# Loads of x from the fifth group on started by ScalarE instead of SyncE

## The reference, cut to what matters

```python
x = x + 0.5 * ffn(layernorm(x))        # ffn: fft over the 512 channels, sparse complex weights, inverse fft, bias
x = x + attn(layernorm(x))             # attn: layernorm, a long causal convolution over time (s4d), residual,
                                       #       layernorm, fc1, gelu, fc2, residual
x = x + 0.5 * ffn(layernorm(x))
```

## Time and profile before

| what | value |
|---|---|
| time, median of 3 runs | 2082.71 us (2082.7, 2082.71, 2084.4) |
| time of the profiled execution | 2079.76 us |
| its span (first to last instruction) | 2078.0 us |
| PE busy | 1893.0 us (91%) |
| DVE busy | 1390.8 us (67%) |
| POOL busy | 970.0 us (47%) |
| ACT busy | 918.9 us (44%) |
| DMA | 210.63 MB, mean 101 GB/s |
| mean granted TensorE clock | 0.97 of full |

### The profile page before, as it was taken

The page is one execution under the profiler, slowest core; times in us unless marked ns, Lnnn a source line. Parts: engine busy times, 40 slices in busy tenths (PEclk is TensorE's granted clock), DMA queues, the critical chain, the costliest instruction groups (busy, mean ns, idle before and its releaser), DMA issues.

```text
span 2078.0 us, 34662 instructions
## 1 busy us (share of the span) xinstructions
PE 1893.0 (91%) x12416; PEld 1185.6 (57%) x12416; DVE 1390.8 (67%) x2456; ACT 918.9 (44%) x1509; POOL 970.0 (47%) x690
## 2 busy tenths in 40 slices
PE   7866677589966999999999999999999999999999
PEld 6433333267645576665756657475665757656574
DVE  4777899867884667656566665657666566665663
ACT  3555677855654243332433424253342424433250
POOL 0665777654443353443535434353543425444351
PEclk9988999889987999999999999999999999999999
DMA  7154233249994223143232323323132232313321
GB/s 254 61 220 177 110 121 122 69 136 283 262 348 119 56 62 67 51 77 97 62 62 57 76 57 78 82 62 63 56 78 65 74 77 62 70 48 77 76 41 41
DMA packets 282956, 210.63 MB, mean 101 GB/s; under 512 B 193058, under 2 KB 227490, under 8 KB 280995
## 3 DMA queue, kind: packets, MB, share of 16 engines
q1 hardware_dynamic: 282788, 208.35, 36.0%
HBM read 103.97 MB, written 66.56 MB: 82 GB/s over the span
## 4 chain that ended last, share of the span: by engine, by line
PE 75%; DVE 9%; DMA 5%; issue 5%; POOL 2%; ACT 2%; SPq 1%; DVEq 0%; ACTq 0%; POOLq 0%
PE psum L1888 32%; PE psum L1844 28%; PE psum L1751 8%; DMA arena<-in_x 3%; PE psum L1802 3%; PE psum L1793 1%; PE psum L1714 1%; DVE bn L1173 1%; DVE arena L1335 1%; DVE bn L1343 1%; PE psum L1811 1%; DVE ring L1389 1%; SPq L496 1%; DVE taps L1307 1%; POOL arena L662 1%
## 5 line engine op out<-in xcount | busy, mean ns | idle before, releaser
L1888 PE MATMUL psum<-arena 128*128 128x512 f16 x3072 | 668.3, 379 | 0.0
L1844 PE MATMUL psum<-arena 128*128 128x256 f16 x5376 | 599.5, 274 | 43.7 <-DMA arena<-taps 33.3
L1844 PEld LDWEIGHTS psum<-arena 128*128 128x128 f16 x5376 | 525.8, 98 | 120.7 <-issue 45.7
L1888 PEld LDWEIGHTS psum<-arena 128*128 128x128 f16 x3072 | 300.3, 98 | 355.9
L1751 PE MATMUL psum<-m_parts,taps 128*128 128x512 f16 x1536 | 354.1, 386 | 80.3 <-DVE taps L1307 78.7
L766 POOL TENSOR_SCALAR arena<-ring,sc 128x512 f16<-128x512 f32 x192 | 297.9, 1563 | 158.5 <-ACT ring L1016 153.1
L642 POOL TENSOR_TENSOR va<-va,mhalf 128x4 f32<-128x4 f32 x79 | 86.7, 1101 | 546.4 <-DVE va L1166 530.5
L1751 PEld LDWEIGHTS psum<-m_parts,taps 128*128 128x128 f16 x1536 | 149.4, 99 | 259.4 <-issue 95.6
L1030 ACT ACTIVATE ring<-psum 128x256 f32<-128x256 f32 x96 | 36.8, 383 | 362.9 <-PE psum L1844 352.6
L1609 DVE SCALAR_TENSOR_TENSOR arena<-ring,sc,arena 128x512 f16<-128x512 f32 x192 | 177.5, 924 | 11.8 <-POOL arena L766 11.8
L766 POOL TENSOR_SCALAR arena<-spare,sc 128x512 f16<-128x512 f32 x64 | 99.2, 1562 | 182.5 <-ACT spare L1016 180.5
(11 more groups left out here) (193 smaller groups left out, 2423.1 us busy)
## 6 DMA issues: line engine op xcount, KB each, us to landing
arena<-in_x SPq DMA_DIRECT2D x16, 1024.0 KB, 9.8
x_scratch<-arena SPq DMA_DIRECT2D x16, 1024.0 KB, 4.3
taps<-taps_copies SPq DMA_DIRECT2D x64, 256.0 KB, 4.1
y_scratch<-arena SPq DMA_DIRECT2D x32, 512.0 KB, 6.0
arena<-y_scratch SPq DMA_DIRECT2D x15, 1024.0 KB, 5.8
arena<-x_scratch SPq DMA_DIRECT2D x15, 1024.0 KB, 5.5
out<-arena SPq DMA_DIRECT2D x15, 1024.0 KB, 4.4
taps<-taps_copies SPq DMA_DIRECT2D x64, 128.0 KB, 4.4
```

The costliest lines, as they stand in the source:

```text
L1844: last = pe.matmul(chain(p), w1_sb[i][:, a, k, p * P:(p + 1) * P], gt[:, 4 * i + 2 * b + k, :], start=start and n == 0, stop=stop and n == ...
L1888: last = pe.matmul(bank(4 + j % 2), hid[:, a, hc, j * P:(j + 1) * P], w2_sb[:, b, hc, :], start=(p == 0 and not lower and n == 0), stop=(p ...
```

## The change

The `load` function of SyncE is gone, with its calls; the two instructions that were in it besides the waits are now issued by ScalarE, directly behind line 927 of a group's fourth tile, for groups 0 to 11. ScalarE waits for its own `u_norm` of that tile, adds to `gate`, waits for the landing of the group's store, and starts the load of the group four later into the same buffer. SyncE keeps its stores and its copies of the taps, which now follow each other with only the wait for `x1_ready` between them.

```diff
-            def load(g, quad, q):
-
-                sp.wait_ge(u_norm, 4 * g)
-                sp.sem_inc(gate, 1)
-                sp.wait_ge(x1_stored[(q - 1) % 4], 16 * ((quad if q else quad - 1) + 1))
-                sp.dma_start(xbuf[(q - 1) % 4], rows(x, g + 3)).then_inc(x_loaded[(q - 1) % 4], 16)
-
             sp.wait_ge(taps_stored, 32)
             store(0, 0, 0)
             copy_taps(0)
             for g in range(1, 4):
                 store(g, 0, g)
-                load(g, 0, g)
                 copy_taps(g)
             with sp.Fori(1, QUADS - 1) as quad:
                 for q in range(4):
                     store(4 * quad + q, quad, q)
-                    load(4 * quad + q, quad, q)
             store(GROUPS - 4, QUADS - 1, 0)
-            load(GROUPS - 4, QUADS - 1, 0)
...
                     act.activation(uring[:, t.j, :], xbuf[t.q][:, t.j, :], ACT.Identity,
                                    scale=va[:, 7, t.j:t.j + 1], bias=ubias[:, t.j:t.j + 1]).then_inc(u_norm, 1)
+                    if t.j == GT - 1 and not (isinstance(t.g, int) and t.g + 4 >= GROUPS):
+                        act.wait_ge(u_norm, 4 * t.g + 4)
+                        act.sem_inc(gate, 1)
+                        act.wait_ge(x1_stored[t.q], 16 * t.quad + 16)
+                        act.dma_start(xbuf[t.q], rows(x, t.g + 4)).then_inc(x_loaded[t.q], 16)
```

## The result

| | before | after |
|---|---|---|
| median of 12 runs each | 2082.69 us | 2078.34 us |
| profiled execution: span | 2078.0 us | 2074.0 us |

The ratio of after to before is 0.9982, with a 95% interval of 0.9973 to 0.999: a gain of 3.7 us, between 2.1 and 5.6. The interval excludes 1, and the gain is just under the 0.2% that the prediction took as its bound. The forecast was 2082.2, a gain of 0.5. Three executions further down were far slower than the rest of their kernel (4999 us of `copy_first`, 2829 us of `pad_act`, 9155 us of `after_sp_equal`, whose only trace is of that one), and no ratio counts them.

A forecast was written before the change was run, and what follows sets the result against it. Four DMA engines serving copy, store and load one after the other were taken to bound the first half. Terms -0.5 + 0 on 2079.76 gave 2079.3; with the median 2.95 us higher, the forecast was 2082.2 us, range 2073 to 2090.

The forecast's parts named there:

- Four engines bound the first half: Taps copies, 115 to 230 us: four DMA engines serve copy, store and load in turn; DVE waits 31.3 us.
- Piece by piece, so 0.5 us a landing and not adding up: Four slow loads: engines alternate queues one piece at a time; each lands 0.5 us sooner, gains not adding up.
- SyncE's part costs and gives nothing; copy 1's issue becomes short: SyncE loses twelve loads: gain nothing, as nobody waits for it; copy 1 follows store 1 at 119.8 us, issue short.
- ScalarE's step, 0.7 us under a cover of 1.56: ScalarE behind line 927: wait, count, registers and issue cost 0.7 us twelve times, hidden in 1.56 us idle; term 0.
- Sum, -0.5 us: Whole launch: -0.5 + 0 on an execution of 2079.76 us gives 2079.3; forecast median 2082.2 us.
- the change does not touch it: Last stage, 1438 of 2078.0 us: unaffected by the change; x stage shifts reach the launch's end one for one.
- Rival one: Taps copies: load passes the copy, DVE's waits go, ScalarE waits for stores; 8.4 us gained, 2074.3; chance 0.23.
- Rival two: Taps copies: copy passes the load, first landing near 167 us; +13 us, 2095.7; chance 0.11.
- Rival three: ScalarE's wait and issue exceed 1.56 us of cover; at 2.1 us the price is 6 us, 2088.7; chance 0.11.
- Rival four: DMA engines serve one transfer's whole share before changing queues; each load lands 2.55 us sooner, 2080.1; chance 0.12.
- within 0.2%: Whole launch: time changes by no more than 0.2%, 4.2 us, indistinguishable from no change; chance 0.53.

The follow-up runs named there:

- copy_first: Kernel before, with SyncE's copy of the taps put between store and load in groups 1 to 3; ratio 1.0114, 23.7 us slower.
- pad_act: Kernel before, loads still on SyncE, ScalarE given a wait for its own u_norm and three semaphore counts behind line 927 of each group's fourth tile; ratio 0.9997.
- after_sp_equal: Changed kernel with 25 counts on the idle semaphore in SyncE's stream, restoring its old 550 instructions, loads staying on ScalarE; ratio 0.9999.
- one_act_dma: Kernel before with only the load of log_dt begun by ScalarE instead of SyncE, every load of x staying on SyncE; ratio 1.0011.
- wide_before: Kernel before with each copy of the taps cut so its slowest dimension is 16 instead of 4, same bytes and order; ratio 0.9859.

## Why the prediction was right, and where it was not

- *Four engines bound the first half.* Right: spread over 16, the copies cost DVE nothing, and 29 us go, of the 31 that it waited.
- *Piece by piece, so 0.5 us a landing and not adding up.* Right in mechanism and size: the windows show pairs of 65 + 2 KB, and the four landings are 0.6 to 0.8 us earlier. That this reaches the end of the launch one for one did not show: the last stage began 0.3 us later than before.
- *SyncE's part costs and gives nothing; copy 1's issue becomes short.* Right within the stage (0.61 us for 10.63). It is the step that failed for the launch as a whole.
- *ScalarE's step, 0.7 us under a cover of 1.56.* 0.92 us, covered: the steady groups stay at 18.0. The waits, the count and the address registers took 0.42 us where the prediction had 0.2, half of it from no row.
- *Sum, -0.5 us.* Measured -3.7 (-5.6 to -2.1). The failed sentence is "the change does not touch it", of the last stage. It does no work there, but PE's pauses at the five jumps back came out 2.6 us shorter and a stretch at half clock, worth 1.6 us, was gone, so the stage is 4 us shorter. That the cause is the 25 instructions fewer in SyncE's stream is shown by one kernel's time (`after_sp_equal`); how they do it is open. The prediction read PE as busy for 1421.74 of 1438 us "at full clock" and did not ask what the other 16 were; over half of them are these pauses, and the mean of 1.00 hid the 3.4 us at half clock.
- *Rival one* did not happen with 65 KB pieces, and did with 4 KB ones, ScalarE's waits for the stores included. *Rival two* is real when one queue holds both, and its price was 23.7 us, not 13. *Rival three* did not happen. *Rival four*, longer turns, is excluded by the windows.
- The forecast of "within 0.2%" held, by a thin margin: a gain of 0.18%, and the interval reaches 0.27%. That it held is partly luck: the term that it rests on, 0.5 us, is the smaller part of what was measured.

## What to carry to other kernels

A transfer that is slow at a fixed spacing is held by something ahead of it: look how many DMA engines that something uses (a share of 0.25 is four of sixteen) before moving the issue to another engine. Here one changed dimension of the copies was worth 29 us, in either kernel (2050.4 and 2050.7 us against 2079.4), and the moved loads at most 0.7. And when two programs differ by 0.2%, look for pauses and for the clock where loops jump back: here 25 instructions in the stream of an engine that was not under test went with more time than the change under test.

## What the runs showed that I had not expected

- A second queue does let a transfer past one in progress, but one piece against one piece: beside 65 KB pieces a 2 KB piece waits 2.4 us, and the first load of 1024 KB took 20.9 us; beside 4 KB pieces the four loads took 11.7 to 12.2.
- Issuing a copy took SyncE 10.63, 7.25 and 7.85 us when a store and a load stood in the queue between it and the copy before, and 0.6 when only a store did.
- A row cut into 128 contiguous parts of 4 KB still ran in pieces of 65,280 bytes; walked backwards it ran in pieces of 4080.
- The length of an engine's instruction stream (25 of 550 on SyncE) went with 0.2% of the time, in a stage in which PE's pauses are not put down to that engine.
- Of the five pauses of PE the kernel before has one followed by half clock (2.11 us), `one_act_dma` one and `wide_before` three (1.98 to 2.07 us); the seven traced kernels with 525 or 565 instructions have none in their loop. Each such stretch lasts 3.4 us and makes its block of matmuls 1.6 us longer. Pauses of 2.03 us in `wide_before` and 2.10 us in `one_act_dma` had none behind them, so the length of the pause alone does not decide it.
